# Two layers of a graph network on one core: ten steps' rows of each round fetched by SyncE, a shorter ring, and the weight work of round 0 five turns later

## The reference

```python
x = layernorm(x + L0(x, src, dst)); x = layernorm(x + L1(x, edge_attr_64, src, dst))
# L0: out[n] = max over edges e with dst[e] == n of
#     relu((x[dst] - x[src]) @ theta_w.T + theta_b + x[src] @ phi_w.T + phi_b), 0 without edges
# L1: hv = x @ W_in + b_in
#     twice: m = relu(concat(hv[src], he) @ W_u + b_u)
#            hv = hv + segment_max(m, dst) where the node has an edge
#     return relu(hv @ W_ro + b_ro)
```

## Time and profile before

| | |
|---|---|
| median of 3 runs | 3835.89 us (3832.41 to 3838.9) |
| the profiled execution: its time | 3804.41 us |
| its span, first to last instruction | 3802.4 us |
| mean granted clock of TensorE | 0.833 of full |
| PE busy | 2669.6 us, 70% |
| DVE busy | 1454.3 us, 38% |
| ACT busy | 200.2 us, 5% |
| POOL busy | 2377.3 us, 63% |
| gathers of edges' rows, line 590 | 2296 from the tables, 38 + 12 from x |
| DMA | 762.04 MB, 200 GB/s in the mean |

### The profile page before, as it was taken

How to read it: one execution, slowest core, us unless ns; L and a number is a source line. 1 busy time by engine, 2 the same in 40 slices (tenths; PEclk the granted TensorE clock), 3 DMA queues, 4 the chain that set the end, 5 groups by cost and what they waited for, 6 DMA issues and landing times.

```text
span 3802.4 us, 24361 instructions
## 1 busy us (share of the span) xinstructions
PE 2669.6 (70%) x6466; PEld 1262.9 (33%) x6466; DVE 1454.3 (38%) x3424; ACT 200.2 (5%) x447; POOL 2377.3 (63%) x2508
## 2 busy tenths in 40 slices
PE   4865666666565757778777777676788777777776
PEld 3632222222222523333333333252333333333334
DVE  0454454445445513323333333321333333333336
ACT  1100000000000500000000000010000000000004
POOL 5456666666664466666666666456666666666644
PEclk7977677676776878998988898887888888888888
DMA  5545555555554646666666666565666656666653
GB/s 200 183 154 184 197 201 201 196 193 195 182 189 150 208 151 219 219 217 224 209 210 206 221 224 211 174 224 173 207 221 227 226 201 218 233 221 222 214 189 124
DMA packets 261238, 762.04 MB, mean 200 GB/s; under 512 B 54675, under 2 KB 107774, under 8 KB 224622
## 3 DMA queue, kind: packets, MB, share of 16 engines
q0 software_dynamic: 120048, 327.78, 28.9%
q1 hardware_dynamic: 87678, 353.79, 23.4%
q10 hardware_dynamic: 53376, 78.93, 6.6%
HBM read 413.88 MB, written 346.40 MB: 200 GB/s over the span
## 4 chain that ended last, share of the span: by engine, by line
PE 52%; another core or an unknown queue 21%; DVE 11%; issue 11%; DVEq 1%; ACT 1%; DMA 1%; POOL 1%; SPq 0%; ACTq 0%; POOLq 0%
PE edge_ps L869 17%; PE edge_ps L867 17%; DVE hist L415 9%; PE edge_ps L846 9%; PE edge_ps L762 4%; PE side_ps L762 3%; PE edge_ps L770 2%; DVE junk L346 1%; DVEq L345 1%; DVEq L413 1%; POOL gath L590 0%; PE side_ps L880 0%; PE edge_ps L880 0%; ACT x_sb L702 0%
## 5 line engine op out<-in xcount | busy, mean ns | idle before, releaser
L590 POOL DMA_INDIRECT gath<-table,src_sb x2296 | 2176.3, 948 | 1196.7 <-issue 618.4
L415 DVE SCALAR_TENSOR_TENSOR hist<-hist,lift,edge_ps 128x256 f32<-128x256 f32 x2346 | 1125.4, 480 | 2052.6 <-remote 989.7
L867 PE MATMUL edge_ps<-w_e,he_sb 128*128 128x512 f32 x1564 | 924.5, 676 | 513.6 <-DVE hist L415 340.4
L869 PE MATMUL edge_ps<-gath,ident 128*128 128x512 f32 x1564 | 888.0, 649 | 36.5 <-issue 24.5
L846 PE MATMUL edge_ps<-gath,ident 128*128 128x512 f32 x732 | 510.3, 827 | 355.9 <-DVE hist L415 268.9
L867 PEld LDWEIGHTS edge_ps<-w_e,he_sb 128*128 128x128 f32 x1564 | 305.2, 211 | 986.0 <-issue 644.4
L869 PEld LDWEIGHTS edge_ps<-gath,ident 128*128 128x128 f32 x1564 | 328.5, 211 | 467.5 <-issue 447.6
L846 PEld LDWEIGHTS edge_ps<-gath,ident 128*128 128x128 f32 x732 | 165.2, 250 | 629.1 <-DVE hist L415 409.2
L660 ACT COPY hv_sb<-side_ps 128x256 f32<-128x256 f32 x147 | 54.8, 373 | 3237.1 <-remote 2615.7
L617 POOL DMA_INDIRECT gath<-runs,end_row x147 | 145.4, 989 | 73.8 <-issue 44.1
L770 PE MATMUL edge_ps<-dst_f,onehot 128*128 128x512 f32 x200 | 91.3, 585 | 29.0 <-DVE onehot L338 20.4
(11 more groups left out here) (136 smaller groups left out, 1142.0 us busy)
## 6 DMA issues: line engine op xcount, KB each, us to landing
runs<-hist SPq DMA_DIRECT2D x285, 1024.0 KB
he_sb<-in_he ACTq DMA_DIRECT2D x194, 256.0 KB
gath<-table,src_sb POOLq DMA_INDIRECT x2296
table<-hist SPq DMA_DIRECT2D x72, 256.0 KB
back_T<-x1T ACTq DMA_DIRECT2D x98, 128.0 KB
runs<-hist SPq DMA_DIRECT2D x33, 256.0 KB
x_sb<-in_x SPq DMA_DIRECT2D x49, 128.0 KB
back_T<-msgT ACTq DMA_DIRECT2D x49, 128.0 KB
```

What stands on the lines that cost most here:

```text
L415: state = V.scalar_tensor_tensor(hist[:, s % H, :], hist[:, (s - 1) % H, :], lift[:, t:t + 1], edges, ALU.add, ALU.max)
L590: pool.indirect_dma_start(gath[:, ring_place(s) % G, :], None, a["x"] if s < RAW else tables[r], bass.IndirectOffsetOnAxis(src_sb[:, t:t + ...
L867: T.matmul(bank, he_sb[:, c % NHE, at:at + P], w_e[r - 1][:, :], start=True, stop=False)
L869: last = T.matmul(bank, ident[:, :], flat(edge_rows(s)), start=False, stop=True)
```

## The change

SyncE takes over the rows of ten steps of each round: the pairs of steps at 152, 288, 424, 560 and 696. Their place is no longer in the ring but in `late_sb`, two buffers of two steps. DVE computes the rows' byte offsets once (`late_at`), SP writes them to DRAM as a list, and before the store of each of the first 80 chunks of a round SP loads 16 offsets into registers and issues 16 transfers of one row of 1 KB each (`late_rows`). POOL skips these steps, and PE waits for 256 landed rows instead of the ring's semaphore. For the memory of the buffers the ring goes from 38 to 34 places, and SPILL from 12 to 16, so RAW stays 50. The weight and bias work of round 0 goes from turns 3 and 4 to turns 8 and 9, and with it the start of the back products, to turn 10. Context is cut from the diff where lines of "..." stand.

```diff
-G, H = 38, 24
+G, H = 34, 24
 SC = 8
...
 XT_FIRST, XT_UNITS = 4, 3
-SPILL, SPILL_TILE = 12, 32
+SPILL, SPILL_TILE = 16, 32
 RAW = G + SPILL
+LATE = 2
+LATE_PAIRS = 5
+LATE_EVERY, LATE_FIRST = 136, 152
+LATE_BUFS = 2
+LATE_PER_CHUNK = 16
+LATE_LOAD = 16
+ROW_BYTES = 4 * D
...
 CONV, NEXT0, NEXT1, OUT = range(4)
-EARLY_TURNS = 3
-WEIGHTS_AT = (EARLY_TURNS + 1) * BODY
+LATE_TURN = 8
+WEIGHTS_AT = (LATE_TURN + 1) * BODY
 FIRST_X_CHUNK = 20
...
+LIST_UNIT = 12
 assert TURNS == TILES and STRIDE % SC == 0 and H % SC == 0 and G % GS == 0 and STRIDE % HC == 0 and HC % GS == 0 and SC % GS == 0
...
     msgT = nc.dram_tensor("msgT", [P, TILES * D], f32, kind="Internal").ap()
+    late_list = nc.dram_tensor("late_list", [LATE_PAIRS, P * LATE], i32, kind="Internal").ap()
+    table_bytes = [t.rearrange("n f -> (n f)").bitcast(mybir.dt.uint8) for t in tables]
     halves = lambda w: w.rearrange("(h k) o -> k h o", h=KH)
...
         fix_rows = sb("fix_rows", [P, D])
+        late_sb = sb("late_sb", [P, LATE_BUFS, LATE, D])
+        late_at = sb("late_at", [P, LATE_PAIRS, LATE], i32)
         fix_T = sb("fix_T", [P, KH, P])
...
         back_kept = sem("back_kept")
+        late_listed = sem("late_listed")
+        late_landed = [sem(f"late_landed{n}") for n in range(ROUNDS * LATE_PAIRS)]
         fix_turned = sem("fix_turned")
...
-        def real(t):
-            return t < STEPS
+        def late_step(n):
+            return LATE_FIRST + n * LATE_EVERY
+
+        def late_pair(t):
+            n, k = divmod(t - LATE_FIRST, LATE_EVERY)
+            return n if 0 <= n < LATE_PAIRS and k < LATE else None
+
+        def by_pool(t):
+            return t < STEPS and late_pair(t) is None
...
             steps = [2 * q if 2 * q < G else 2 * q + SPILL for q in range(at % (G // 2), at + 1, G // 2)]
-            return sum(real(step % STRIDE) for step in steps)
+            return sum(by_pool(step % STRIDE) for step in steps)
...
         def edge_rows(s):
+            r, t = divmod(s, STRIDE)
+            n = late_pair(t)
+            if n is not None:
+                return late_sb[:, (r * LATE_PAIRS + n) % LATE_BUFS, :, :]
             if in_spill(s):
...
-            if r == 0 and i < 2 * (EARLY_TURNS + 2):
-                return range(max(0, 2 * (i - EARLY_TURNS - 2)), max(0, 2 * (i - EARLY_TURNS - 1)))
+            if r == 0 and i < 2 * (LATE_TURN + 2):
+                return range(max(0, 2 * (i - LATE_TURN - 2)), max(0, 2 * (i - LATE_TURN - 1)))
             return range(i, i + 1)
...
             dve.wait_ge(edges_loaded, 16 * len(edge_loads))
+            for n in range(LATE_PAIRS):
+                last = V.tensor_scalar(late_at[:, n, :], src_sb[:, late_step(n):late_step(n) + LATE], ROW_BYTES, None,
+                                       ALU.mult)
+            reached("late offsets", last)
             dve.wait_ge(bits_loaded, 16 * len(edge_bits))
...
                         find_ends(i + 1, node_no[:, 0:1], end_row[:, i:i + 1], float(P))
-                        if i == EARLY_TURNS:
+                        if i == LATE_TURN:
                             bias_columns()
...
+            def late_rows(r, c):
+                total = LATE_PAIRS * P * LATE
+                i, end = min(c * LATE_PER_CHUNK, total), min((c + 1) * LATE_PER_CHUNK, total)
+                while i < end:
+                    n, at = divmod(i, P * LATE)
+                    m = r * LATE_PAIRS + n
+                    count = min(LATE_LOAD, end - i, P * LATE - at)
+                    if i == 0:
+                        for written, k in all_written(staged_written, r + 1):
+                            sp.wait_ge(written, k)
+                        sp.wait_ge(late_listed, 16)
+                    if at == 0 and m >= LATE_BUFS:
+                        was_r, was_n = divmod(m - LATE_BUFS, LATE_PAIRS)
+                        sp.wait_ge(group_summed, groups_to(was_r * STRIDE + late_step(was_n)))
+                    regs = [nc.sync.alloc_register(f"late{r}_{i + k}") for k in range(count)]
+                    nc.sync.load(regs, late_list[n:n + 1, at:at + count])
+                    for k, reg in enumerate(regs):
+                        p, t = divmod(at + k, LATE)
+                        offset = nc.sync.snap(reg, donate=True, min_val=0, max_val=(NPAD - 1) * ROW_BYTES)
+                        sp.dma_start(late_sb[p:p + 1, m % LATE_BUFS, t, :].bitcast(mybir.dt.uint8),
+                                     table_bytes[r][bass.DynSlice(offset, ROW_BYTES)].rearrange("(o f) -> o f", o=1)
+                                     ).then_inc(late_landed[m], 16)
+                    i += count
+
             def store_runs(r):
                 for c in range(CHUNKS):
+                    late_rows(r, c)
                     if r == 0 and 0 <= c - FIRST_X_CHUNK < TILES:
...
                 write_table(0, u)
+                if u == LIST_UNIT:
+                    sp.wait_ge(setup_step, setup_at["late offsets"])
+                    with nc.allow_non_contiguous_dma("small layouts"):
+                        sp.dma_start(late_list.rearrange("n (p k) -> p n k", k=LATE), late_at[:, :, :]
+                                     ).then_inc(late_listed, 16)
             sp.wait_ge(setup_step, setup_at["none row"])
...
             def gather_edges(r):
-                for t in range(STEPS):
+                for t in filter(by_pool, range(STEPS)):
                     s = r * STRIDE + t
...
             def wait_rows(s):
-                pe.wait_ge(slot_filled(s), 2 * 16 * pairs_in_slot(s))
+                r, t = divmod(s, STRIDE)
+                n = late_pair(t)
+                if n is None:
+                    pe.wait_ge(slot_filled(s), 2 * 16 * pairs_in_slot(s))
+                else:
+                    pe.wait_ge(late_landed[r * LATE_PAIRS + n], 16 * P * LATE)
...
                             back(t)
-                    if turn_no == EARLY_TURNS and at == BODY // 2 + GS:
+                    if turn_no == LATE_TURN and at == BODY // 2 + GS:
                         multiply_weights()
```

More of the change, by code:

```diff
@@ L37 @@
 XT_FIRST, XT_UNITS = 4, 3
-SPILL, SPILL_TILE = 12, 32
+SPILL, SPILL_TILE = 16, 32
 RAW = G + SPILL
+LATE = 2
[5 more added lines that the diff above has]
+ROW_BYTES = 4 * D
+assert SPILL % GS == 0 and SPILL_TILE + SPILL <= TILES
 CONV, NEXT0, NEXT1, OUT = range(4)
-EARLY_TURNS = 3
-WEIGHTS_AT = (EARLY_TURNS + 1) * BODY
+LATE_TURN = 8
+WEIGHTS_AT = (LATE_TURN + 1) * BODY
 FIRST_X_CHUNK = 20
-assert SPILL % GS == 0 and SPILL_TILE + SPILL <= TILES
+LIST_UNIT = 12
 assert TURNS == TILES and STRIDE % SC == 0 and H % SC == 0 and G % GS == 0 and STRIDE % HC == 0 and HC % GS == 0 and SC % GS == 0
```

## The result

The changed kernel took 4153.2 us (median of 6 runs, 4136.9 to 4173.3), the kernel before 3836.9 (6 runs, 3822.3 to 3841.8): a ratio of 1.083, 95% interval 1.081 to 1.085. The prediction was 3792. It is slower by 316 us where 44 less were forecast, and beyond the upper end of the range.

A forecast was written before the change was run, and what follows sets the result against it. It took POOL's back-to-back gathers, with stalls scaling with their number, as the bound. Gathers -40, weights -7, ring 0 and bursts of DVE +3 made -44, so 3835.9 became 3792 us; range 3775 to 3860.

The forecast's parts named there:

- the sixteen issues: SyncE's sixteen one-row transfers before a chunk's store, priced from single issues in the earlier trace: 5.8 to 8.3 us.
- the batch: SyncE's register load plus sixteen transfers per chunk: 9.0 to 11.5 us, 9.9 in the middle, hidden if under 10.8.
- The load: SyncE's loading of 16 offsets into registers before each chunk's transfers, charged at 3.2 us.
- The rival that came true: SyncE becomes the bound: batches over 10.8 us delay the stores; about 4030 us at a 12 us batch; chance 0.16.
- The break-even at 11.2 us: The SyncE batch length at which the whole forecast gain of 44 us would be gone.
- the news of a finished sum reaches DVE and POOL late: While POOL gathers back to back, PE's finished sums are seen late, so stalls scale with the number of gathers.
- Gathers removed, -40: Thirty gathers, ten a round, leave POOL; between 37.5 and 42.7 us saved, taken as 40.
- Weights moved, -7: Round 0's weight and bias work moves to turns 8 and 9; gain between 0 and 9.6 us, taken as 7.
- ring, 0: POOL's gather ring shrinks from 38 to 34 places; up to 15 us cost against 10.3 saved, taken as 0.
- The rival that the readers are the bound: POOL's stalls grow as its gathers shrink, leaving only the weights' 7 us: 3829 us; 0.12, shared with late stores.
- one DMA engine takes all the rows: All one-row transfers go to one DMA engine, so gathers and stores land late: 4001 us; chance 0.03.
- Late pairs: PE's waits for SyncE's late rows, fetched at least 20 steps (28 us) earlier: 0 us.

The follow-up runs named there:

- e5: The changed kernel itself, unaltered, on a chip of the quick kind: 3198.8 us against 3253.5 for the kernel before, ratio 0.983.
- e9: The changed kernel with no rows fetched and no register loads, the five pairs left out, on the slower chip kind: 3754.2 us against 3806.6.
- e16: The changed kernel with 16, 8 and 12 rows a chunk in rounds 0, 1 and 2, slower chip kind: 3962.0 us against 3802.5.
- e15: The changed kernel, slower chip kind; round 1 with constant row addresses and no register loads, round 2 without POOL's gathers: 3587.6 us against 3802.5.
- e17: The changed kernel with two late pairs instead of five, 8 rows a chunk, on the slower chip kind: 3783.0 us against 3802.5, ratio 0.995.
- e1: The kernel before with only the ring of 34 and the moved weight work, quick chip kind: 3240.3 us against 3252.7, ratio 0.996.
- e2: The changed kernel with SyncE fetching no row, the five pairs left out of the computation, quick chip kind: 3200.7 us, ratio 0.984.
- e6: The changed kernel with 8 more one-row transfers a chunk from the table to a scratch tensor, quick chip kind: 3920.5 us, ratio 1.206.
- e7: The changed kernel with POOL gathering nothing in rounds 1 and 2, quick chip kind: 2763.5 us, ratio 0.850.
- e13: The changed kernel with POOL gathering nothing in rounds 1 and 2, repeated on the second chip of the quick kind: ratio 0.847.
- e4: The changed kernel with two late pairs instead of five, 8 rows a chunk, quick chip kind: 3224.9 us, ratio 0.992.
- e11: The changed kernel with two late pairs and 8 rows a chunk, repeated on the second chip of the quick kind: ratio 0.991.
- e10: The changed kernel with six late pairs instead of five, 20 rows a chunk, slower chip kind: 4322.7 us against 3806.6.

## Why the prediction was wrong

*The step that failed: the sixteen issues, and so the batch.* The prediction put sixteen issues at 5.8 to 8.3 us and the batch at 9.0 to 11.5, 9.9 in the middle, under a budget of 10.8, and so called it hidden. In the changed kernel the batch was 13.3, 12.1 and 12.4 us in the mean of each round, and not hidden. The load was not the trouble: 3.2 us were charged, it took 1.9. (The Trainium skill, "Runtime: NRT & Kernel Launch", section "Instruction fetch mechanics", gives about 200 ns a register; here 16 registers took 1.9 us in the changed kernel and 2.1 in e5, 0.12 to 0.13 us each, so the measurement is lower.) The transfers were: 15 pitches of 0.67 to 0.76 us are 10.0 to 11.3 us, with 6.1 to 7.4 us of pauses in them. Without pauses, as on A, they are 15 x 0.34 = 5.1 us, and the batch would have fitted. On A the pitch of 0.34 to 0.35 us was below the prediction's lower end of 0.36, and the batch of 7.3 to 7.5 was hidden, as it had it.

The rows that the price came from the earlier trace rows are single issues, and single issues do not show the pauses. Of the 318 stores of `hist` in the kernel before, issued one by one, nearly all while POOL gathered, none took over 0.45 us; in the changed kernel, where a train goes before each, 25 took over 0.65 and 50 under 0.05. The term was mis-sized because a train is not a sum of single issues there.

The bounds had slips of their own. A one-row transfer of 0.35 us with a gap of 0.04 makes 16 x 0.39 = 6.2 us, not 5.8, which is 16 x 0.36, the pitch of the store; and the middle of 9.0 to 11.5 is 10.25, not 9.9. The room was then 0.5 us and not 0.9, which asked for a higher chance of the rival.

*The rival that came true has the right mechanism; that its sum fits is in part luck.* Batches of 13.3, 12.1 and 12.4 us in 80 x (batch - 10.8) - 17.5 give 182.5, 86.5 and 110.5 us, about 380 together, on top of the forecast of 3792: 4172, and 4153 was measured. Round by round the changed kernel lost 228, 67 and 90 us against e9, so the formula is too low in round 0 and too high in the others. The break-even at 11.2 us was a little late: in round 2 of e16 a batch of 10.9 us had already eaten the gain (stretch 1129.1 us, before 1127.2, e9 1114.3). The chance of 0.16 for lying beyond it was too small for a term that no row showed.

*What the trace had told, and I used for one thing only.* The prediction found that while POOL gathers back to back, "the news of a finished sum reaches DVE and POOL late". It charged this to gathers and stalls, and let SyncE issue at the quick rate in the same stretches. e15 shows that both go with the gathers. The chain of waits of e5 and the waits of its DVE between 1500 and 2300 us show that the late news is absent on A, as the pauses are:

```profile
POOL 43%; DMA 18%; PE 17%; issue 16%; DVE 3%; ACT 2%; DVEq 1%; SPq 0%; ACTq 0%; POOLq 0%
```

```profile
DVE hist L444 <- PE edge_ps L933: 421.4, 288, 8.7
```

There is no "unknown queue" in the chain, where the earlier trace rows had 21%, and none of DVE's waits in that stretch is put down to "remote". POOL itself is the bound there. In e17, on B, it is back:

```profile
PE 46%; another core or an unknown queue 23%; DVE 14%; issue 12%; DVEq 2%; ACT 1%; DMA 1%; POOL 0%; SPq 0%; ACTq 0%; POOLq 0%
```

That the late news and the slow issues have one cause is argued from this, not shown.

*Gathers removed, -40: right.* 39.6 us on A (e1 against e2). On A the value comes without any late news, since POOL itself is the bound there; on B only the sum of all small terms was measured. *Weights moved, -7, and ring, 0: right within 6 us.* Together -12.5 on A, and all edits without the batch -52.0 on A and, with one run of each kernel, -52.4 on B, against the -47 of these terms. The wait of DVE for `w_e` is gone from the changed kernel's waits. How much of the 12.5 is the weights and how much the ring was not separated.

*The rival that the readers are the bound did not come true:* e2 and e9 gained more than the 7 us that it left. *Nor did the one that one DMA engine takes all the rows and fills up:* the queue's packets rose by 96014 - 87678 = 8336, about two for each of the 3840 transfers, and on which engines they ran no run shows; but e5 carried the same transfers at no cost, and with e6's 24 a chunk the pace was the sum of the issues and nothing more. *Late pairs:* PE waited for rows of L564 twice, 6.6 us in all; 0 was predicted.

*Round 0 is the worst* (228 us of the 384 between e9 and the change). It has the highest pitch of the three in the changed kernel (10.5 pauses a batch against 8.7 and 8.8) and one more issue a chunk, the load of `x`. Why it has more pauses I have not found.

*Part of the loss is given back.* In the last chunks, where no rows are fetched, the pace was 9.0 to 9.4 us instead of 10.7 to 11.4, since POOL had run on behind the waiting readers: in round 1 its lead over DVE fell from 36 steps at step 640 to 12 at step 760.

## What to carry to other kernels

An idle queue is worth what a train of instructions costs on it in that stretch, beside that work. Before moving work to it, look for signs that the stretch holds other engines up (waits with an unknown releaser, news that comes late). Take the price of an issue from a train of issues there: in the kernel before, single issues in the very same stretch looked quick. Where the sum of issues comes near the pace of the loop, the loss beyond the edge is about 80 times the excess a round, while the gain within it is fixed. So stay inside: 8 rows a chunk gained on each of the three chips that it ran on, 16 gained 1.7% on the quick kind and lost 8% in the comparison. And a term that no row shows, with the sign of the result hanging on it, deserves a chance near even, not one in six.

## What the runs showed of the hardware

- Chips differ by more than the change: the kernel before took 3253 to 3262 us on two and 3803 to 3837 elsewhere, and the sign of the change differed with them. With GpSimd's gathers left out, round 2 took 760.1 us on both kinds (e7, e13, e15). The gathers themselves are issued 1.25 us apart on both. What differs between the chips, and whether it is the issue of the gathers or their traffic, stays open.
- On the slower kind, while GpSimd gathers and about 2 us longer, a train of SyncE's instructions stands still for 0.70 us again and again, 8 to 10 times in a batch of 8 to 20 rows. The pauses show in transfers and in moves between registers: in the changed kernel 15 to 19% of the transfers and 14 to 18% of the moves took over 0.6 us, and in e5 on the other kind up to 2% and none. Stores issued one by one in the kernel before showed none (318, at most 0.44 us).
- A one-row transfer from DRAM to SBUF with its address in a register is issued every 0.32 us in a quick stretch, 0.23 of it the transfer; a one-row transfer between two tensors in DRAM took 0.63 (e6). A register load took 0.9 to 1.2 us in the mean for 8 registers (e16, e17; e4, e11), 1.7 to 2.2 for 16 and 2.3 to 2.4 for 20 (e10).
